# A graph network on one core: own rows scaled on two engines in the attention passes, messages kept in SBUF in the node passes

## The reference

```
h = relu(layernorm(x));  x = x + GAT(h)
h = relu(layernorm(x));  x = x + GNN(h)
GAT, 3 layers, every node has an edge to itself as well:
  e = leaky_relu((hW a_src)[src] + (hW a_dst)[dst]);  alpha = softmax of e over the edges of one dst
  h = h + sigmoid(segment_sum(alpha * (hW)[src], dst) + b)
GNN, 3 layers:
  e   = relu([h[src], h[dst], e] @ We + be)        # the first layer has no e
  agg = segment_sum(e * edge_weight, dst)
  h   = relu([h, agg] @ Wn + bn)
```

## Time and profile before

| | us |
|---|---|
| median of three runs | 6092.61 (6088.71 to 6099.74) |
| the profiled execution | 6093.98 |
| its span | 6092.1 |

### The profile page before, as it was taken

The page is one execution under the profiler, slowest core; times in us unless marked ns, Lnnn a source line. Parts: engine busy times, 40 slices in busy tenths (PEclk is TensorE's granted clock), DMA queues, the critical chain, the costliest instruction groups (busy, mean ns, idle before and its releaser), DMA issues. The chain is left out here.

```text
span 6092.1 us, 100401 instructions
## 1 busy us (share of the span) xinstructions
PE 5122.6 (84%) x23996; PEld 3034.7 (50%) x23996; DVE 4340.3 (71%) x11924; ACT 3412.1 (56%) x7493; POOL 3450.1 (57%) x3533
## 2 busy tenths in 40 slices
PE   4999999999994768837773888799989997777785
PEld 2666666666651234424442444466656664333332
DVE  7888888888864799958885999555545544544443
ACT  4888888888874857736662677433323322222222
POOL 3544444444412557347755774477566654777777
PEclk9999999999997978868886999899999999999887
DMA  9999997777655867636664898676677774444442
GB/s 220 311 299 303 302 293 246 239 239 246 223 182 174 252 176 221 197 114 199 201 198 126 277 294 280 194 212 209 188 217 221 221 216 142 136 130 127 129 130 84
DMA packets 909508, 1274.03 MB, mean 209 GB/s; under 512 B 248502, under 2 KB 398967, under 8 KB 902579
## 3 DMA queue, kind: packets, MB, share of 16 engines
q1 hardware_dynamic: 696170, 1063.92, 53.0%
q0 software_dynamic: 112896, 202.19, 14.2%
q10 hardware_dynamic: 100016, 3.20, 1.2%
HBM read 623.49 MB, written 654.07 MB: 210 GB/s over the span
## 5 line engine op out<-in xcount | busy, mean ns | idle before, releaser
L1734 POOL DMA_INDIRECT n_xs<-table,look x1176 | 1116.1, 949 | 695.9 <-issue 318.2
L1439 POOL DMA_INDIRECT g_xs<-table,look x784 | 777.7, 992 | 454.5 <-issue 234.1
L1873 DVE TENSOR_TENSOR_SCAN n_dT<-n_km,n_dT,bank 128x512 f32<-128x512 uint8 x291 | 372.3, 1279 | 549.8 <-PE bank L1761 549.8
L626 POOL DMA_INDIRECT p_rows<-in_x_dram,dst_ix x392 | 389.1, 993 | 486.5 <-DMA raw_rows<-p_rows 259.0
L634 POOL DMA_INDIRECT table<-slot_pair,map_ix x392 | 396.0, 1010 | 457.0 <-ACT n_sg L742 249.2
L670 PE MATMUL bank<-n_xT,gat_w 128*128 128x512 f32 (+1 forms) x1176 | 542.8, 597 | 18.0 <-ACT n_xT L734 16.0
L689 PE MATMUL bank<-n_zT,wn 128*128 128x512 f32 (+1 forms) x1176 | 539.2, 594 | 6.6 <-ACT n_zT L734 6.6
L1746 POOL DMA_INDIRECT out_dram<-n_xn,n_row_of x392 | 385.6, 984 | 141.0 <-issue 118.2
L1838 ACT ACTIVATE n_eT<-bank,edge_b 128x512 f32<-128x512 f32 x294 | 201.7, 686 | 430.5 <-PE bank L1778 430.2
L1557 ACT ACTIVATE g_xw<-g_xs,g_cols 128x128 f32<-128x128 f32 x1176 | 370.6, 386 | 76.7 <-PE bank L1507 49.3
L1855 ACT ACTIVATE n_xn<-bank 128x512 f32<-128x512 f32 x98 | 58.5, 597 | 613.3 <-DMA out_dram<-n_xn,n_row_of 606.5
(11 more groups left out here) (275 smaller groups left out, 12462.6 us busy)
## 6 DMA issues: line engine op xcount, KB each, us to landing
table<-n_ro SPq DMA_DIRECT2D x768, 256.0 KB
g_gb<-decays SPq DMA_DIRECT2D x294, 256.0 KB
n_xd<-table SPq DMA_DIRECT2D x294, 256.0 KB
table<-g_xn SPq DMA_DIRECT2D x196, 256.0 KB, 4.2
g_xo<-table SPq DMA_DIRECT2D x196, 256.0 KB
edge_feats<-n_eT SPq DMA_DIRECT2D x196, 256.0 KB
table<-n_xn SPq DMA_DIRECT2D x196, 256.0 KB
n_ea<-edge_feats SPq DMA_DIRECT2D x196, 256.0 KB
```

Source lines behind the costliest of these rows:

```text
L626: q.indirect_dma_start(out=edge_rows[e % UX][:, u, :], out_offset=None, in_=x, in_offset=bass.IndirectOffsetOnAxis(ap=dst_ix[:, t:t + 1], ...
L1439: q.indirect_dma_start(out=xs[g % XR][:, u, :], out_offset=None, in_=tables[l], in_offset=bass.IndirectOffsetOnAxis(ap=src_ix[:, t:t + 1] ...
L1734: q.indirect_dma_start(out=xs.buffers[g % UE][:, u, :], out_offset=None, in_=tables[L], in_offset=bass.IndirectOffsetOnAxis(ap=look[:, t, ...
L1873: V.tensor_tensor_scan(in_order(dT[g][:, :]), kept(g), in_order(flat_banks[1]), 0.0 if begins(g) else carry(dT[g.before(1)]), ALU.mult, AL ...
```

## The change

The GAT passes: ScalarE, after its four scalings of gathered tiles, waits for the own rows and multiplies the last two of the four tiles by column 1 into a new ring `so` of two buffers. VectorE keeps its scale-and-add for the first two tiles (`UA = 2`), and adds the other two in one `tensor_tensor` of 256 columns. SP's `load_own` stands at lag 14 instead of 15.

The first two GNN passes: `messages` writes into a new SBUF ring `mT` of two buffers, and `totals` reads it from there. The bank of the norm product is free again after `messages`, so `weights` waits for `msg` and not for `total`; and it stands ahead of `nodes` in TensorE's list. The third GNN pass stays as it is.

```diff
+            UA = 2
+                so = of_ring(f"g{l}_so", 2, (P, UA, P), c=c2)
                         def add_self(g):
                             v.wait_ge(scaled, g + 1)
                             landed(v, ol, g)
-                            for u in range(U):
-                                last = V.scalar_tensor_tensor(out=xw[g % 3][:, u, :], in0=xo[g % OR][:, u, :],
-                                                              scalar=column(g, 1, u), in1=xw[g % 3][:, u, :],
-                                                              op0=ALU.mult, op1=ALU.add)
-                            last.then_inc(selfed, 1)
+                            for u in range(U - UA):
+                                V.scalar_tensor_tensor(out=xw[g % 3][:, u, :], in0=xo[g % OR][:, u, :],
+                                                       scalar=column(g, 1, u), in1=xw[g % 3][:, u, :],
+                                                       op0=ALU.mult, op1=ALU.add)
+                            V.tensor_tensor(xw[g % 3][:, U - UA:U, :], xw[g % 3][:, U - UA:U, :], so[g % 2][:, :, :],
+                                            ALU.add).then_inc(selfed, 1)
...
-                                  (9, store_decays), (17, load_decays), (15, load_own)]
+                                  (9, store_decays), (17, load_decays), (14, load_own)]
...
                             for u in range(U):
-                                last = S.activation(xw[g % 3][:, u, :], xs[g % XR][:, u, 0:C], ACT.Copy, scale=column(g, 0, u))
+                                S.activation(xw[g % 3][:, u, :], xs[g % XR][:, u, 0:C], ACT.Copy, scale=column(g, 0, u))
+                            landed(a, ol, g)
+                            ready(a, selfed, g - 1)
+                            for u in range(U - UA, U):
+                                last = S.activation(so[g % 2][:, u - U + UA, :], xo[g % OR][:, u, :], ACT.Copy,
+                                                    scale=column(g, 1, u))
                             last.then_inc(scaled, 1)
...
+                mT = None if last_layer else ring("mT", 2, (P, P * U))
+                def messages_of(g):
+                    return norm_of(g) if last_layer else mT[g][:, :]
...
                         def weights(g):
-                            after(pe, total, g, NR)
+                            after(pe, total if last_layer else msg, g, NR)
...
-                            pipeline(pe, GE, [(4, enter), (7, nodes), (5, weights), (5, edges)], UE)
+                            pipeline(pe, GE, [(4, enter), (5, weights), (7, nodes), (5, edges)], UE)
...
-                            V.tensor_tensor(norm_of(g), norm_of(g), eT[g][:, :], ALU.mult).then_inc(msg, 1)
+                            V.tensor_tensor(messages_of(g), norm_of(g), eT[g][:, :], ALU.mult).then_inc(msg, 1)
...
-                            V.tensor_tensor_scan(in_order(aT[g][:, :]), kept(g), in_order(norm_of(g)),
+                            V.tensor_tensor_scan(in_order(aT[g][:, :]), kept(g), in_order(messages_of(g)),
```

## The result

The changed kernel takes 6034.55 us (median of four runs, 6028.76 to 6041.77) against 6094.4 us (four runs, 6088.71 to 6099.74) of the kernel before on the same chip: a ratio of 0.9903, 95% interval 0.9885 to 0.992. The profiled execution took 6035.81 us (span 6034.0). The forecast was 6025, in a range of 5998 to 6082.

What follows compares the result with a forecast made beforehand. Bounds: VectorE in the first and, in its window, third GAT pass, POOL's gathers in the second, TensorE in both GNN passes. From 6093.98 us, -20 (GAT), -20 and -29 (GNN) made -69, so 6025; range 5998 to 6082.

Steps and rivals of the forecast that it cites:

- Islands on TensorE: First two GNN passes: adjacent bf16 products leave one island of gaps instead of two, 0.30 us a group, 29 us each pass.
- Rival 2: First two GNN passes: gaps belong to each bf16 product, so these passes stay as they are; 6074 us, chance 0.08.
- The message scan holds gathers: First two GNN passes, POOL: SBUF message scan can hold one gather a group; first pass gains 20 us, second full 29.
- Rival 1: First GNN pass: gather loop falls into its slow phase, +78 us instead of -20; 6123 us, chance 0.12.
- VectorE's addition: GAT passes: one 256-column addition lasts 0.40 us, 0.33 counted without overlap, replacing two scale-and-adds of 0.263 each.
- First GAT pass -13: VectorE gains 0.19 us in 87 groups, -17; end +3.4 at 0.43 a group more, low clock +1.
- Third GAT pass -10: VectorE is the bound for 60 groups, 0.19 us each, -11; low clock +1; nothing for the end.
- Second GAT pass +3: Gathers bound this pass, so only its end counts, where ScalarE becomes the bound: +3 us.
- ScalarE's load and waits, the own load one place earlier: GAT passes: two more scalings, 0.58 us a group, hidden by ScalarE's idle while VectorE bounds; own load costed at nothing.
- Rival 3: GAT passes: ScalarE takes VectorE's place as the bound, no gain there; 6045 us, chance 0.12.
- the attention half: The change in the three GAT passes: together -20 us, bounds -49 to +13.
- the GNN half: The change in the first two GNN passes: -20 us in the first, -29 in the second.

Runs made afterwards that it cites:

- Kernel 10: Kernel before plus the change's GAT part, with the GNN bias product moved behind the node products, directly ahead of the norm product; 6030.89 us, ratio 0.9886.
- kernel 6: Changed kernel, but the messages of the first two GNN passes stay in their PSUM bank, the new product order kept; 6031.19 us, ratio 0.99.
- kernel 4: Changed kernel, but the second GAT pass as before: no own rows scaled on ScalarE, four scale-and-adds on VectorE; 6013.24 us, ratio 0.9864.
- kernel 8: Changed kernel, but in the second GAT pass ScalarE scales all four tiles and VectorE adds them in one 512-column addition; 6050.6 us, ratio 0.9917.
- kernel 9: Changed kernel, but VectorE does its four scale-and-adds as before, while ScalarE still scales two tiles that nobody reads; 6045.04 us, ratio 0.9915.

## Why the prediction came out right, and which terms did not

The mechanism of the larger half was right to a tenth of a microsecond; in the other half one term, the second GAT pass, came out at four to six times its forecast, because VectorE's edit there was costed at nothing.

- **Islands on TensorE, 0.30 us a group in each GNN pass.** Right: 0.29 in both by the periods, 26.8 and 26.3 us by the stages. Kernel 10 shows it from the other side. Rival 2, a gap for each product, is out.
- **The message scan holds gathers; 9 us of the first pass's 29 taken off for it.** The hold-up is real (48 of 392 gathers over 1.0 us there, 87 of 392 in the second pass, up to 1.92), but costs nothing: kernel 6 without it takes 525.4 us, against 525.3. So the 9 us were taken off for nothing. TensorE waited 7.3 us for gathered rows over the whole first pass, in four waits. Caught were fewer than one in four: one in eight in the first pass. Rival 1 did not come about.
- **VectorE's addition 0.40 us, 0.33 counted.** Right: 0.41 lasting.
- **First GAT pass -13.** -8.4; over ten profiles with this code against two without, -8.5. The end cost 0.32 a group instead of 0.43, and in VectorE's waits 5.9 us stand for gathered rows that come late, where there were none. These waits come late in the pass, from 372 us on. The mean gather on that pass's table rose from 0.981 to 1.162 us (264 of them), so POOL's lead ran out.
- **Third GAT pass -10.** -14.6, and -14.2 over the same ten. I had counted the gain for 60 groups only and taken the first part of the pass for bound by gathers. The starts of the scans show the lead growing evenly from group 7 (0.2 us) to group 87 (14.8), 0.18 us each. Why the first part gains as well, though VectorE waits for some gathers there, wasn't tried.
- **Second GAT pass +3.** This is the term that failed: "gathers bound it, so only its end counts". That gathers bind the pass was right, and just therefore it was wrong to cost VectorE's edit at nothing. I weighed the hold-up where the change visibly turned a PSUM input into an SBUF one, and forgot that the new `tensor_tensor` is itself an operation on two SBUF tensors, in the one pass where POOL has no slack: +18.6 us in the pair of profiles, 12 by the mean of five profiles each, 19 by the medians of all executions, by VectorE's addition (kernels 4, 8 and 9). Of this some 3 us are the end that had been costed (0.32 for each of eight groups).
- **ScalarE's load and waits, the own load one place earlier.** Hidden, as costed: ScalarE waited 0.3 us for own rows in the first pass. Rival 3 did not come about.

So the attention half gave 7 us where I wrote 20, the GNN half 52 where I wrote 49. That the time came within 10 us of the forecast has luck in it: by the stages of the table the second GAT pass missed by 16 us and the first by 5, and the third GAT pass (5) and the first GNN pass (7, as its hold-up cost nothing) missed the other way and hid half of that.

The Trainium skill, SBUF — State Buffer, section Who interferes with whom, says that a VectorE instruction with two SBUF inputs contends with a GpSimd instruction that reads SBUF. The trace agrees for additions, scans and new rows, and for scale-and-adds in part: of the gathers that start 0.08 to 0.12 us after one of these, 59 of 61 are held, of those that start earlier 14 of 188. So the number of inputs alone doesn't give the price; it has to be read from the trace of the very instruction.

## What to carry to other kernels

Where one engine binds a stage, a change on another engine isn't free until it has been asked what that engine does to the binding one: here an addition that saved VectorE 0.19 us cost POOL more. On a TensorE that is always busy, put the products of odd shape next to each other; each island of them cost 0.3 us here, in three parts of about 0.1. And try a change stage by stage: its best version here is the one that leaves it out of the stage with another bound.

## What the runs showed of the hardware

- A gather that is held by VectorE's operation on two SBUF tensors ends 0.82 to 0.84 us after that operation. Of 27 that started with the first of two `tensor_tensor` in a row, 14 were let in after the first (1.05 to 1.08 us) and 13 only after the second (1.24 to 1.28). What decides between the two stays open.
- The scale-and-add with its factor from a column (128 columns, two SBUF tensors) holds a gather too, but only one that starts 0.08 us or more after it, and mostly to its own end (1.07 us); one that starts within 0.07 us after it mostly passes (0.94). The addition of 256 columns holds that one every time (1.20). The earlier trace rows show the same instruction with a constant factor on 512 columns: its gather started 0.04 ahead of it and was held for 0.58. Why they differ stays open; width, factor and operation weren't varied singly.
- A held gather can set up the next hold: 25 of 48 long ones after, 2 of 25 before. In its second pass the kernel took 596 to 603 us with the same instructions; that the chain of holds is what varies was not tried, but the sum of the holds varies with it (24 to 31 us).
- The 0.3 us that an island of small products costs TensorE does not depend on its place (kernels 6 and 10), and two of them next to each other cost no more than one (0.22 and 0.23 us from one to the next, no gap). The Trainium skill, TensorEngine Tiling (Array Packing), section Key Properties, says that changing the tiling mode drains TensorE; no row here tells in which mode the products of 3 and 7 rows ran.
